# One gather of sixteen moved from GpSimd to 128 row-by-row DMAs of SyncE, for every fourth tile

## The reference

```python
x = x + gnn0(layernorm(x), adj);  x = x + ffn0(layernorm(x));  x = x + gnn1(layernorm(x), adj)
# last layer, for each of 2048 rows and each of 8 heads, with layernorm(x) as x:
q   = x @ Wq * 128**-0.5
sim = [q_pk[p] @ pk_keys[p].T for p in (0, 1)]            # two times 128 scores
scores, idx = top_k(sim, 16)                              # 16 of each half
score = scores[0][:, None] + scores[1][None, :]           # 256 pairs
final, pk = top_k(score, 16);  index = idx[0] + 128 * idx[1] at pk;  w = softmax(final)
k = sum_16(w * keys_table[index + head * 16384])          # rows of 128 floats
v = sum_16(w * values_table[index + head * 16384])
out = softmax(causal(q @ k.T)) @ v                        # over all 2048 rows
x = x + concat_heads(out) @ Wo
```

## Time and profile before

| | us |
|---|---|
| median of 3 runs (lowest, highest) | 2874.64 (2873.76, 2875.33) |
| the profiled execution, its own time | 2873.7 |
| its span | 2871.8 |
| busy: TensorE matmul, VectorE, GpSimd, ScalarE | 2220.4, 1865.3, 1960.1, 779.9 |
| mean granted share of TensorE's clock | 0.927 |

### The profile page before, as it was taken

How to read it: one execution, slowest core, us unless ns; L and a number is a source line. 1 busy time by engine, 2 the same in 40 slices (tenths; PEclk the granted TensorE clock), 3 DMA queues, 4 the chain that set the end, 5 groups by cost and what they waited for, 6 DMA issues and landing times. The chain is left out here.

```text
span 2871.8 us, 39679 instructions
## 1 busy us (share of the span) xinstructions
PE 2220.4 (77%) x11458; PEld 1784.0 (62%) x11458; DVE 1865.3 (65%) x6336; ACT 779.9 (27%) x2032; POOL 1960.1 (68%) x2064
## 2 busy tenths in 40 slices
PE   6858578887788777886778777876788767886777
PEld 6848566765666556665566655665566656665565
DVE  6689777767666656666566665666666656666641
ACT  5746422221122112221223112221223112221122
POOL 0003767777777777777777777777777777777774
PEclk9969889999899989999999889999999899999999
DMA  4201333333333333333333333333333333333332
GB/s 162 97 1 33 94 94 105 109 106 106 105 108 106 106 106 108 106 107 105 106 108 107 106 106 108 106 107 105 106 108 107 106 106 108 106 107 105 106 105 77
DMA packets 109591, 292.33 MB, mean 102 GB/s; under 512 B 34129, under 2 KB 41809, under 8 KB 107345
## 3 DMA queue, kind: packets, MB, share of 16 engines
q0 software_dynamic: 98304, 268.57, 32.6%
q1 hardware_dynamic: 10080, 20.97, 2.1%
q10 hardware_dynamic: 1008, 0.33, 0.0%
HBM read 288.69 MB, written 1.05 MB: 101 GB/s over the span
## 5 line engine op out<-in xcount | busy, mean ns | idle before, releaser
L295 POOL DMA_INDIRECT ring<-table,rows x2048 | 1952.6, 953 | 717.9 <-issue 586.0
L1504 PE MATMUL ps<-ring,staged 128*128 128x256 f32 x4096 | 1019.7, 406 | 229.3 <-DMA ring<-table,rows 209.8
L1504 PEld LDWEIGHTS ps<-ring,staged 128*128 128x128 f32 x4096 | 813.1, 202 | 404.6 <-DMA ring<-table,rows 263.0
L773 DVE RECIPROCAL prec<-psum_row 128x1 f32<-128x1 f32 x128 | 20.9, 164 | 541.4 <-DVEq L772 541.0
L1141 ACT ACTIVATE work<-ps 128x256 f32<-128x256 f32 x128 | 49.0, 383 | 1054.0 <-ACTq L1139 1054.0
L1580 PE MATMUL ps<-s2w,work 128*128 128x128 f32 x2176 | 307.9, 289 | 34.0 <-PEq L1578 33.1
L1580 PEld LDWEIGHTS ps<-s2w,work 128*128 128x128 f32 x2176 | 276.0, 200 | 65.7 <-issue 62.6
L765 DVE TENSOR_REDUCE nmax<-ps 128x1 f32<-128x128 f32 (+7 forms) x127 | 162.7, 1281 | 205.9 <-DVEq L764 205.8
L1549 PE MATMUL ps<-work,qT 128*128 128x512 f32 (+3 forms) x576 | 244.2, 554 | 67.6 <-PEq L1541 64.8
L758 DVE TENSOR_TENSOR staged<-ps,wgt 128x2048 f32<-128x2048 f32 x128 | 291.9, 2281 | 0.2 <-issue 0.2
L1567 PE MATMUL ps<-ident,work 128*128 128x128 f32 x1088 | 194.1, 304 | 39.9 <-PEq L1560 21.0
(11 more groups left out here) (241 smaller groups left out, 2488.2 us busy)
## 6 DMA issues: line engine op xcount, KB each, us to landing
ring<-table,rows POOLq DMA_INDIRECT x2048, 2.8
staged<-adj_in SPq DMA_DIRECT2D x16, 1024.0 KB, 4.8
xs<-x_in SPq DMA_DIRECT2D x4, 256.0 KB, 6.7
wpkq<-w_pkq SPq DMA_DIRECT2D x8, 128.0 KB
out<-xs SPq DMA_DIRECT2D x1, 832.0 KB, 4.7
keyd<-pk_keys SPq DMA_DIRECT2D x16, 32.0 KB
wo<-w_o SPq DMA_DIRECT2D x8, 64.0 KB, 2.1
out<-xs SPq DMA_DIRECT2D x1, 192.0 KB, 2.1
```

The lines of the kernel that those rows point to most:

```text
L295: nc.gpsimd.indirect_dma_start(ring[:, t % RING, k, :], None, table_d, bass.IndirectOffsetOnAxis(ap=rows[:, t % ROWS, k:k + 1], axis=0),). ...
L1504: ins = m.matmul(to, diag(t)[:, k, :], ring[:, t % RING, k, :], start=(k == 0), stop=(k == TOPK - 1))
```

## The change

For tiles 3, 7, 11 and 15 of each head (in head 0 only 7, 11 and 15), GpSimd issues 15 gathers in place of 16. The sixteenth is done in another way:

- VectorE writes the row numbers of such a tile to a tile of its own, `rowl`, besides `rows`, and raises `rowl_full`.
- TensorE transposes the sixteenth column of `rowl` (128 numbers to one row), in steps 0, 4, 8 and 12, after `project` and before the sums (`turn_offsets`).
- ScalarE copies that row out of PSUM, times 1024, as integers: byte offsets into the table (`offsets_out`).
- SyncE loads 32 of them into registers at a time and issues one DMA of 1 KB for each, 128 for the tile (`fetch_rows`).
- The last of the 16 matmuls of the sums of such a tile waits for all 128 (`rows_in_sem`). The last gather of tile 15 had a semaphore of its own before; that one is gone.
- The weights of the next head are loaded by ScalarE: `wpkq` and `keyd` in step 10 behind `project_out`, `wo` in step 1 of the new head behind `turned_out(0)`.

```diff
+def by_rows(t, first):
+    return t % RING == RING - 1 and not (first and t == RING - 1)
...
@@ sync
-            with sp.Fori(1, HEADS) as h:
-                sp.wait_ge(head_used, 1)
-                load_head(h)
-                sp.wait_ge(wo_used, 1)
-                sp.dma_start(wo[:, :], wo_d[h]).then_inc(wo_in, 16)
+            def fetch_rows():
+                sp.wait_ge(offs_sb, 1)
+                sp.sem_inc(offs_sb, -1)
+                for c in range(0, P, LOADED):
+                    _, at = nc.values_load_multi_w_load_instructions(
+                        offs[0:1, c:c + LOADED], engines=(mybir.EngineType.SP,), min_val=0, max_val=(HEADS * NKV - 1) * ROW_BYTES,
...
+                    for i in range(LOADED):
+                        sp.dma_start(ring[c + i:c + i + 1, RING - 1, TOPK - 1, :].bitcast(U8),
+                                     table_bytes[:, bass.ds(at[i], ROW_BYTES)]).then_inc(rows_in_sem, 16)
...
@@ gpsimd, gather
-                for k in range(TOPK):
+                for k in range(TOPK - by_rows(t, first)):
...
@@ vector, look_up_5
+                if by_rows(t, first):
+                    dve.sem_inc(rowl_full, 1)
...
@@ scalar
+            def offsets_out():
+                act.wait_ge(offs_full, 1)
+                act.sem_inc(offs_full, -1)
+                s.activation(offs[:, :], ps[0:1, 2, 0:P], ACT.Copy, scale=float(ROW_BYTES)).then_inc(offs_sb, 1)
...
+                if t + AHEAD + 1 == T - 1 and not last:
+                    load_head(h + 1)
+                if t % RING == 0 and not (first and t == 0):
+                    offsets_out()
...
+                if t == 1 and not first:
+                    act.wait_ge(wo_used, 1)
+                    act.sem_inc(wo_used, -1)
+                    act.dma_start(wo[:, :], wo_d[h]).then_inc(wo_in, 16)
...
@@ tensor, sums
-                        if t == T - 1 and k == TOPK - 1:
-                            pe.wait_ge(last_in, h * 16 + 16)
+                        if by_rows(t, first) and k == TOPK - 1:
+                            pe.wait_ge(rows_in_sem, 16 * P)
+                            pe.sem_inc(rows_in_sem, -16 * P)
...
+            def turn_offsets():
+                pe.wait_ge(rowl_full, 1)
+                pe.sem_inc(rowl_full, -1)
+                m.transpose(ps[0:1, 2, 0:P], rowl[:, TOPK - 1:TOPK], ident[:, :]).then_inc(offs_full, 1)
...
+                if t % RING == 0 and not (first and t == 0):
+                    turn_offsets()
```

More of the change, by code:

```diff
@@ L12 @@
 U32 = mybir.dt.uint32
+U8 = mybir.dt.uint8
 ALU = mybir.AluOpType
@@ L248, in _ @@
             sp.dma_start(wo[:, :], wo_d[0]).then_inc(wo_in, 16)
-            with sp.Fori(1, HEADS) as h:
-                sp.wait_ge(head_used, 1)
-                sp.sem_inc(head_used, -1)
-                load_head(h)
-                sp.wait_ge(wo_used, 1)
-                sp.sem_inc(wo_used, -1)
-                sp.dma_start(wo[:, :], wo_d[h]).then_inc(wo_in, 16)
+            table_bytes = table_d.rearrange("r d -> (r d)").bitcast(U8).rearrange("(o n) -> o n", o=1)
+            def fetch_rows():
[4 more added lines that the diff above has]
+                        offs[0:1, c:c + LOADED], engines=(mybir.EngineType.SP,), min_val=0, max_val=(HEADS * NKV - 1) * ROW_BYTES,
+                        skip_runtime_bounds_check_because="row numbers are sums of a head's offset and two positions")
+                    for i in range(LOADED):
+                        sp.dma_start(ring[c + i:c + i + 1, RING - 1, TOPK - 1, :].bitcast(U8),
+                                     table_bytes[:, bass.ds(at[i], ROW_BYTES)]).then_inc(rows_in_sem, 16)
+            for t in range(T):
+                if by_rows(t, True):
+                    fetch_rows()
+            with sp.Fori(1, HEADS):
+                for t in range(T):
+                    if by_rows(t, False):
+                        fetch_rows()
             sp.wait_ge(out_ready, 1)
@@ L286, in _, with gather @@
                 nc.gpsimd.tensor_tensor(part, part, bffn[:, :].unsqueeze(1).to_broadcast([P, GT, D]), ALU.add).then_inc(bias_ok, 1)
-            def gather(t):
+            def gather(t, first):
                 pool.wait_ge(rows_full, 1)
@@ L297, in gather @@
                         bass.IndirectOffsetOnAxis(ap=rows[:, t % ROWS, k:k + 1], axis=0),
-                    ).then_inc(last_in if t == T - 1 and k == TOPK - 1 else gathered[t % RING][k // QK], 16)
-            with pool.Fori(0, HEADS):
+                    ).then_inc(gathered[t % RING][k // QK], 16)
+            for t in range(T):
+                gather(t, True)
+            with pool.Fori(1, HEADS):
                 for t in range(T):
-                    gather(t)
+                    gather(t, False)
         @block.vector
@@ L739, in look_up_3, with row_numbers, look_up_4, look_up_5 @@
                                 cand_ps.unsqueeze(1).to_broadcast([P, TOPK, NCAND]), ALU.mult)
[L741 to L745, removed]
+            def row_numbers(t, first):
+                return rowl if by_rows(t, first) else rowf
+            def look_up_4(t, first):
+                v.tensor_reduce(row_numbers(t, first)[:, :], pick[:, :, :], X, ALU.add)
+            def look_up_5(t, first):
+                if by_rows(t, first):
+                    dve.sem_inc(rowl_full, 1)
+                v.tensor_copy(rows[:, t % ROWS, :], row_numbers(t, first)[:, :]).then_inc(rows_full, 1)
             def weigh_1(t):
@@ L830, in step @@
                 if find:
-                    find_all(a)
+                    find_all(a, first and t < T - AHEAD)
                 if last and t == T - 1:
@@ L1481, in _, with landed, per @@
             operands_ready()
-            def landed(h, t, q):
-                per = [16 * (QK - (q == QUARTERS - 1 and s == T - 1)) for s in range(t % RING, T, RING)]
-                pe.wait_ge(gathered[t % RING][q], h * sum(per) + sum(per[:t // RING + 1]))
+            def landed(h, t, q, first):
+                def per(first):
+                    return [16 * (QK - (q == QUARTERS - 1 and by_rows(s, first))) for s in range(t % RING, T, RING)]
+                if first:
+                    pe.wait_ge(gathered[t % RING][q], sum(per(True)[:t // RING + 1]))
+                else:
+                    pe.wait_ge(gathered[t % RING][q], (h - 1) * sum(per(False)) + sum(per(True)) + sum(per(False)[:t // RING + 1]))
             def bank1():
@@ L1492, in kv_copied, with sums @@
                 pe.sem_inc(kv_full, -1)
-            def sums(h, t, quarters, to=kv_ps):
+            def sums(h, t, quarters, first, to=kv_ps):
                 for q in quarters:
@@ L1511, in _ @@
             bank1()
-            sums(0, 0, range(QUARTERS))
+            sums(0, 0, range(QUARTERS), True)
             group(3)
@@ L1618, in step @@
                     bank1()
-                    sums(h, 0, range(QUARTERS))
+                    sums(h, 0, range(QUARTERS), False)
                     kv_copied()
@@ L1623, in step @@
                         bank1()
-                    sums(h, t, range(QUARTERS))
+                    sums(h, t, range(QUARTERS), first)
                     exponentials()
```

51 lines of the change are left out of this document (30 added, 21 removed).

## The result

The changed kernel took **2838.2 us** (median of four runs, 2835.7 to 2838.9) where the kernel before took 2874.6 (four runs, 2873.8 to 2875.3): a ratio of 0.9875, 95% interval 0.9863 to 0.9887. That is 36.4 us faster. The forecast was 2980 and slower. The time lies just inside its range of 2834 to 3400, but it is the time of rival A (2836), in which SyncE keeps up.

What follows compares the result with a forecast made beforehand. SyncE's row-fetch loop was to replace GpSimd as the bound: a period of 83.5 against 80.0 us before, 30 intervals each 3.5 longer, so 105 us on the profiled 2873.7 gave 2979, as median 2980; range 2834 to 3400.

Steps and rivals of the forecast that it cites:

- rival A: SyncE keeps up with the row fetches and all 38.8 us are gained: 2836 us, chance 0.29.
- GpSimd sets the pace at 1.25 us a gather: GpSimd bounds the kernel before; 31 gathers removed save 38.8 us if nothing else takes over.
- The loop P = S + L + c: SyncE's fetch, TensorE's work and hand-overs run in series from fetch to fetch: period 83.5 us, 13.5 of it beyond the fetch.
- L: TensorE's work from the end of a fetched tile's sums to the end of `project` in the next step: mean 10.1 us.
- Landing and last matmul: After a fetch's last issue: 2.1 us to land, then 0.4 us for the two passes of the last matmul.
- the crossing: SyncE's time per fetch below which GpSimd stays the bound and the full gain comes: 65.2 us.
- the forecast's S of 70: SyncE's time to fetch one tile: 58.9 issues, 8.4 register loads, 2.7 stalls; 70.0 us, ends 49 and 115.
- S = 58.9 for the issues: SyncE's 128 row DMAs of a tile at 0.46 us each: 58.9 us, ends 49 and 88.
- The stalls, 2.7: SyncE's issues delayed at instruction-queue packets, 4 in each fetch at 0.68 us: 2.7 us.
- The loads, 8.4: SyncE's four register loads of 32 offsets per tile, each one memory trip of 2.1 us: 8.4 us, ends 0.2 and 24.
- rival C: SyncE's loads cost per register (0.19 us a value, 3460) or rows cost 0.69 us (3850); over 3280, chance 0.19.
- The weights on ScalarE's queue, nothing, 17 + 14 without cover: Moved weight loads cost nothing behind TensorE's gather waits; uncovered, 17 us for `wo` and 14 us for step 10.

Runs made afterwards that it cites:

- e11: Changed kernel with five tiles a head by rows in place of four, and doubled row-number, offset and landing buffers: 2827.8 us, ratio 0.9841 to the kernel before.
- e6: Changed kernel with 48 more row DMAs in each fetch, into a spare tile, also waited for by the last matmul: 2960.7 us, ratio 1.0305 to the kernel before.
- e7: Changed kernel with 96 more row DMAs in each fetch, into a spare tile, also waited for by the last matmul: 3449.8 us.
- e10: Changed kernel with each row DMA cut into 16 pieces of 60 bytes: 3698.1 us.
- e9: Kernel before with trains of plain DMAs of 1 to 128 rows added to SyncE's queue, before the heads and in heads 1 to 7: 2873.0 us.
- e5: Changed kernel with 16 register loads of 8 values for each tile in place of 4 loads of 32: 2839.8 us.
- e12: Kernel before with only the next head's weight loads moved to ScalarE's queue: 2874.5 us, ratio 1.0000.

## Why the prediction was wrong, point by point

**GpSimd sets the pace at 1.25 us a gather.** Right: 38.1 of 38.8 us came at the last gather, and eight more removed (e11) gave 10.4 us of 10.0 expected, about their full price.

**The loop P = S + L + c.** The mechanism is right, and its wait sized a little low: 15.1 against 13.5 (e6, e7, e10). The term that was low is L, 12.0 in e7 where four places of before gave 10.1. In the changed kernel, which has slack, tiles 3, 7 and 11 still give 6.9, 8.8 and 11.0, as in the forecast, and in the bound loop of e7 on the mean 10.1, 10.5 and 12.5. So rows read where TensorE has slack did not hold where it has none; why, is open. Landing and last matmul together were right in sum (2.4 against 2.5) and wrong in their parts (1.2 and 1.2 against 2.1 and 0.4). Its count was off too: the whole is 31 S and not only 30 intervals against GpSimd's. Both move the crossing from 65.2 to 62.8. With the forecast's S of 70 the span would have been 414 + 2170 + 452 + 22 = 3058, so at an S of 70 the sum would have been 80 us too low.

**S = 58.9 for the issues.** This is the step that failed: the term of the sum that prices one row at 0.34 + 0.12 = 0.46 us. "DMAs alone in SyncE's queue take 0.33 to 0.35 us, with 128 rows": the price was taken from DMAs of 64 to 128 rows, and so was its low end, 0.38. A DMA of one row takes 0.225 and 0.318 with all around it: 128 x 0.318 = 40.7, 18 us less than the sum and 8 under its low end. The gap of 0.12 between issues was nearly right (0.093, of which the register's MOVE is 0.029). By the measured sum S with 0.46 a row would be 58.9 + 8.5 = 67.4 us and over the crossing of 62.8, so this one term turned the sign. Shown by e9 (0.29 for one row, 0.46 for 16, in a train on the same queue) and by e10.

**The stalls, 2.7.** They did not come for one-row DMAs: 0.433 us is the longest of 3968, and in e9 none of 105 pairs was over 0.25 us late. The 14 issues of before were all `keyd` loads of 64 rows. The shape alone does not explain their stalls: in the same execution of e9 six of the 14 `keyd` loads took 0.97 to 1.60 us, and of 49 pairs of 64 rows in the trains behind them one was late. Nor does a packet of the instruction queue, at which all six lay: 181 of the 3968 one-row DMAs lay across one too, and none took over 0.433 us. Why those stall and these don't is open.

**The loads, 8.4.** Right in size, 4 x 2.12 = 8.5, and that by luck: the forecast took a load as one trip to memory of 2.1 us, and e5 shows 0.78 for 8 values, so the price goes with the values and meets 2.1 only at 32 of them. The price per value is 0.056 us, far under rival C's 0.19. By the Trainium skill (Runtime: NRT & Kernel Launch, Instruction fetch mechanics), with about 200 ns a register even in bulk, a load of 32 would take 6.4 us, as an estimate. The trace does not agree for these values in SBUF: 2.12 us. So both grounds for rival C are gone. S = 40.7 + 8.5, and 1.3, nearly all for rows later than the median, is 50.5, where the forecast had 70.0.

**The weights on ScalarE's queue, nothing, 17 + 14 without cover.** Right in cause and size. The three loads of step 10 hold ScalarE's queue for 1.8 to 2.7 us (forecast 1.5 to 2.5). TensorE's wait in front of the product with `wo` is 87.3 us where it was 69.9:

```profile
PE ps L1597 <- PEq L1596: 69.9, 128, 0.8
```

17.4 us, 7 x 2.5; one such wait stands in TensorE's timeline of the changed kernel at step 1:

```profile
1284.40 0.46 PE L1658 MATMUL ps<-wo,oT 128*128 128x128 f32 x2 [2.71 <-PEq L1657]
...
1327.60 1.99 PE L1565 MATMUL ps<-ring,staged 128*128 128x256 f32 x8 [3.02 <-DMA ring<-table,rows]
```

The cover named in the forecast is there, the wait of 3.02 us for tile 3's gathers further down, and e12 shows that nothing of such a wait is left in the time.

**Many small transfers.** The Trainium skill (DMA: Bandwidth & Descriptors, Rules for kernel authors) would have them coalesced. Here 128 issues of 40.7 us stood in a queue with nothing else to do, and the engine that bounds the kernel lost one of its own for each tile. So the result of this case, 36 us faster, does not go with the rule: it counts the transfer's cost, not whose time it is.

**The chances.** Rival A's own condition was written down: 0.38 a row, or 0.44 and cheap loads. The forecast treated the low end of an issue, read from other shapes, as a limit. The row of the kernel before that was nearest in bytes (1 KB a row) was far in shape (one row against 128). That the time fell inside the range is owed to rival A, whose 2836 the range was stretched to reach, and not to the loop as forecast. Two of the forecast's own signs of being wrong came: SyncE waits 27 us between fetches, where over 14 was to mean that GpSimd is still the bound, and the pitch of a row, 0.318, lies under its low end of 0.38.

## What to carry to other kernels

Price an issue from a DMA of the same shape, and where the trace has none, let the low end of the range lie well under the nearest row: here one row cost about two thirds of what 128 rows did (0.29 against 0.47 in the trains), and that alone turned the sign. Write a chain between two engines as start + n x work + (n - 1) x hand-over + tail before comparing it with the other engine's sum, and give the crossing from that. An idle queue can take work from the bound engine as long as its waits stay visible between the pieces: four and five tiles a head paid nearly full price, at six the queue was full, and the waits that had been free before became the loss.

## What the runs showed of the hardware

- The price of an issue in SyncE's queue, start to start in a train: 0.29 us for 1 and 2 rows, 0.34 for 4 and 8, 0.46 for 16 (rows of 1 KB); 0.64 for 64, 1.80 for 127 and 0.47 for 128 (rows of 256 B). With its address from a register one row takes 0.32 from start to start, and cut into 16 pieces 0.63 (e10).
- A register load of 32 values from SBUF takes 2.12 us and one of 8 takes 0.78; from these two, as an estimate, 0.34 and 0.056 per value.
- TensorE's granted clock in the last 48 us of the profiled execution was 0.92 in the changed kernel, and 0.98 in the last 46 before, with the same count of its instructions; TensorE was busy 2.5 us longer there. Eight passes at the same place took 3.46, 5.03, 5.13, 5.16 and 6.52 us in different runs (before and e9; e12; e11; the changed kernel; e5).
